# First attention of a four-layer hybrid: the outputs' guard in four passes, two copies on another engine, the queries' rounding and three other steps at other places in the order

## The reference, cut to what matters

```python
h = nan_to_num(layernorm(x), nan=0, posinf=1e4, neginf=-1e4)
Q, K, V = heads(h @ wq.T), heads(h @ wk.T), heads(h @ wv.T)      # 16 heads of 16
Q, K = Q * cos + rotate_half(Q) * sin, K * cos + rotate_half(K) * sin
scores = where(first 25 or last 128 keys, Q @ K.T / 4, lowest)
probs = softmax(scores)
# a gate from the last query's row adds one value to the last values
out = (probs @ V) @ wo.T
x = x + nan_to_num(out, nan=0, posinf=1e4, neginf=-1e4)
```

## Time and profile before

| | us |
|---|---|
| runs, median (lowest to highest of 3) | 941.94 (941.64 to 942.05) |
| the profiled execution | 944.91 |
| its span in the trace | 942.9 |
| busy in the span: TensorE / VectorE / ScalarE / GpSimd | 856.5 / 717.7 / 531.3 / 434.7 |

### The profile page before, as it was taken

How to read it: one execution, slowest core, us unless ns; L and a number is a source line. 1 busy time by engine, 2 the same in 40 slices (tenths; PEclk the granted TensorE clock), 3 DMA queues, 4 the chain that set the end, 5 groups by cost and what they waited for, 6 DMA issues and landing times.

```text
span 942.9 us, 19230 instructions
## 1 busy us (share of the span) xinstructions
PE 856.5 (91%) x6286; PEld 649.1 (69%) x6286; DVE 717.7 (76%) x2366; ACT 531.3 (56%) x1392; POOL 434.7 (46%) x683
## 2 busy tenths in 40 slices
PE   6678898889999999987999999999999997999996
PEld 5556666667765666655888787887888775666663
DVE  6567988889778887663968787787868686888872
ACT  5356544454354555545676676757586761555555
POOL 0348898887766665446202121221202012556655
PEclk9779999999999999989999999999999999999999
DMA  6333333332223557102112020202021022234331
GB/s 211 60 50 49 53 56 55 56 55 38 35 37 58 103 118 133 43 14 46 24 24 46 1 46 1 45 2 46 2 45 37 11 35 35 36 71 59 59 48 35
DMA packets 49938, 46.55 MB, mean 49 GB/s; under 512 B 5280, under 2 KB 47280, under 8 KB 49840
## 3 DMA queue, kind: packets, MB, share of 16 engines
q1 hardware_dynamic: 49840, 45.33, 26.2%
HBM read 11.40 MB, written 2.10 MB: 14 GB/s over the span
## 4 chain that ended last, share of the span: by engine, by line
PE 33%; DVE 15%; issue 3%; ACT 1%; POOL 1%; DMA 0%; POOLq 0%; SPq 0%; DVEq 0%; ACTq 0%
PE bank L301 8%; PE bank L1979 6%; PE bank L1987 4%; PE bank L1913 4%; DVE weights L1476 3%; PE bank L1928 3%; DVE weights L1466 3%; PE bank L1743 2%; PE bank L1756 2%; DVE q_lo L1456 1%; PE bank L1739 1%; DVE rope L1454 1%; PE bank L1782 1%; DVE xn L338 1%; DVE arena L1313 1%
## 5 line engine op out<-in xcount | busy, mean ns | idle before, releaser
L1313 DVE TENSOR_REDUCE arena<-bank 128x2 f32<-128x512 f32 (+1 forms) x192 | 130.9, 685 | 42.4 <-PE bank L1743 41.4
L924 ACT ACTIVATE weights<-bank 128x512 f32<-128x512 f32 x144 | 85.8, 596 | 109.1 <-PE bank L1756 108.3
L1006 ACT ACTIVATE weights<-weights,neg_max 128x128 f32<-128x128 f32 (+1 forms) x256 | 113.9, 449 | 39.2 <-DVE neg_max L1466 38.7
L727 POOL TENSOR_SCALAR_AFFINE_SELECT weights<-weights 128x256 f32<-128x256 f32 x144 | 68.6, 478 | 101.4 <-ACT weights L924 101.4
L1979 PE MATMUL bank<-kbT,arena 128*128 128x128 f32 (+1 forms) x512 | 105.1, 328 | 1.0 <-DVE y L447 0.9
L667 POOL TENSOR_SCALAR weights<-weights 128x512 f32<-128x512 f32 x64 | 97.6, 1537 | 12.5 <-ACT weights L832 12.5
L1743 PE MATMUL bank<-kf_stack,q_stack 96*128 96x256 f32 (+1 forms) x256 | 99.7, 432 | 0.0
L1013 ACT ACTIVATE weights<-bank 128x384 f32<-128x384 f32 x128 | 62.7, 490 | 61.0 <-PE bank L1987 60.5
L1466 DVE CUSTOM_DVE_ANT_0 weights<-bank,arena 128x128 f32<-128x128 f32 (+1 forms) x256 | 80.2, 350 | 14.6 <-PE bank L1979 12.6
L301 PE MATMUL bank<-x_hi,wb_hi 128*128 128x256 f32 x256 | 83.8, 327 | 2.8 <-DVE q_lo L1456 2.8
L1476 DVE TENSOR_SCALAR weights<-weights,inv_sum 128x128 f32<-128x128 f32 (+1 forms) x256 | 81.3, 360 | 4.6
(11 more groups left out here) (236 smaller groups left out, 2514.2 us busy)
## 6 DMA issues: line engine op xcount, KB each, us to landing
q_stack<-q_hi SPq DMA_DIRECT2D x96, 128.0 KB, 4.5
arena<-arena SPq DMA_DIRECT2D x64, 128.0 KB, 2.5
q_stack<-q_lo SPq DMA_DIRECT2D x48, 128.0 KB, 5.3
ka_stack<-k_hi SPq DMA_DIRECT2D x32, 76.5 KB, 2.8
x_all<-x SPq DMA_DIRECT2D x8, 256.0 KB, 5.1
st_wo<-b_wo SPq DMA_DIRECT2D x8, 256.0 KB, 4.2
arena<-b_wqn SPq DMA_DIRECT2D x8, 256.0 KB, 3.3
out<-x_all SPq DMA_DIRECT2D x8, 256.0 KB, 2.1
```

Source lines behind the costliest of these rows:

```text
L924: a.activation(s["pT"][(STEPS * b + k) % N_PT], p2[k % 2][:, :], ACT.Exp).then_inc(s["exp"], 1)
L1006: last = a.activation(p, p, ACT.Exp, scale=-1.0, bias=neg_max[:, h % 4, t:t + 1], accum_out=sums[:, h % 4, t:t + 1])
L1313: v.tensor_reduce(into, p1[k % 2][:, :].rearrange("p (s g k) -> p s g k", s=n, g=NC), AX.X, ALU.max, negate=True).then_inc(s["maxed"], 1)
```

## The change

Eight edits, all in the first attention:

1. The outputs' guard has four passes: the first clamps the bank to +-1e4 into `guard_z`, the second makes max(min(p, 0), `guard_z`) into `guard_t`, the third makes the mask from the bank, the fourth copies the bank where the mask is set. The fourth stands in step 15, the first two in step 13 (step 15 in iteration 9, as before). `ps_r` is held for all four.
2. TensorE's `untranspose_a` and the first `untranspose_f` wait for four passes.
3. The copy into `rep_lo` moves from VectorE to ScalarE, at step 3.
4. The pad of `hT` moves from VectorE to ScalarE, at step 13 ahead of `x_hi`.
5. ScalarE's `high` for the queries moves from step 8 to the end of step 11 for b >= 0.
6. GpSimd's `low` for the queries moves from step 9 to step 12.
7. GpSimd's `residual` moves from step 9 to step 3.
8. SyncE issues `sp_put_shift(b, 0)` at step 10 ahead of the queries' stack, not at step 12 behind it.

Counts and waits of semaphores follow (`guarded` 5 to 4). The core of the diff:

```diff
 # SyncE
+                if k == 10 and there(b):
+                    sp_put_shift(sa, b, 0)
                 if k == 10 and there(b + 1):
                     sp_stack(b + 1, "q")
-                if k == 12 and there(b):
-                    sp_put_shift(sa, b, 0)
 # GpSimd
+                if k == 3 and there(b - 3):
+                    residual(sa, b - 3, guard_t, at(sa, "guarded", b - 3, 4))
-                if k == 9 and b >= 0 and there(b + 1):
+                if k == 12 and b >= 0 and there(b + 1):
                     low(b + 1, "q")
-                if k == 9 and there(b - 3):
-                    residual(sa, b - 3, guard_t, at(sa, "guarded", b - 3, 5))
 # ScalarE
+                if k == 3 and there(b + 1):
+                    act.wait_ge(*at(sa, "x_lo", b + 1, 1))
+                    a.activation(rep_lo[...], x_lo[:, :, 0:VC]..., ACT.Copy).then_inc(sa["rep"], 1)
-                if k == 8 and there(b + 1):
+                if k == 8 and b < 0 and there(b + 1):
                     high(b + 1, "q")
                 if k == 13 and there(b + 2):
+                    act.wait_ge(*at(sa, "hT", b + 2, 2))
+                    act.wait_ge(*at(sa, "x_lo", b + 2, 0))
+                    a.activation(hT[:, :, T:TX], hT[:, :, 0:TX - T], ACT.Copy).then_inc(sa["hT"], 1)
                     act.wait_ge(*at(sa, "hT", b + 2, 3))
-                    act.wait_ge(*at(sa, "x_lo", b + 2, 0))
                 if k % OCT in ITEM_STEPS and there(b - 1):
                     exp_a(b - 1, k // OCT, ITEM_STEPS[k % OCT])
+                if k == 11 and b >= 0 and there(b + 1):
+                    high(b + 1, "q")
 # VectorE
-                link(sa, "guarded", b, 1, v.tensor_scalar(guard_t, ps_r[:, :], 0.0, None, ALU.max))
-                v.scalar_tensor_tensor(guard_z, ps_r[:, :], 0.0, guard_t, op0=ALU.min, op1=ALU.add)\
+                link(sa, "guarded", b, 1, v.tensor_scalar(guard_z, ps_r[:, :], -BIG, BIG, ALU.max, ALU.min))
+                v.scalar_tensor_tensor(guard_t, ps_r[:, :], 0.0, guard_z, op0=ALU.min, op1=ALU.max)\
                     .then_inc(sa["guarded"], 1)
                 if i == 0:
-                    ins = v.tensor_scalar(m, guard_z, 0.0, 0.0, ALU.mult, ALU.is_equal)
-                elif i == 1:
-                    ins = v.tensor_scalar(guard_t, guard_z, -BIG, BIG, ALU.max, ALU.min)
+                    ins = v.tensor_scalar(m, ps_r[:, :], 0.0, 0.0, ALU.mult, ALU.is_equal)
                 else:
-                    ins = v.copy_predicated(guard_t, m, guard_z)
+                    ins = v.copy_predicated(guard_t, m, ps_r[:, :])
-                if k == 3 and there(b + 1):
-                    repeat_lo(b + 1)
-                if k == 6 and there(b - 3):
-                    guard_inf(b - 3, 2)
-                if k == (14 if b <= B else 15) and there(b - 2):
-                    guard_nan(b - 2)
+                if k == (13 if b <= B else 15) and there(b - 2):
+                    guard_nan(b - 2)
 # TensorE
-                    wait_since(pe, sa, "guarded", b - 1, 2)
+                    wait_since(pe, sa, "guarded", b - 1, 4)
```

More of the change, by code:

```diff
@@ L155, in hybrid_layers_kernel @@
                      e_dve=11, e_exp=3, v_ps=1, v_big=1, v_small=1, b_ps=1, v_done=1, rep=2, s_ps=H, maxed=H,
-                     clamped=2, sT_ps=2 * ITEMS, exp=2 * ITEMS, guard=8, guard_first=2, yT_ps=1, yT=1, wo_ps=NT, guarded=5)
+                     clamped=2, sT_ps=2 * ITEMS, exp=2 * ITEMS, guard=8, guard_first=2, yT_ps=1, yT=1, wo_ps=NT, guarded=4)
         sf = [signals("ffn", "f", **TURNED, q_ps=1, kg_ps=2, k_sel=3, k48=3, kT_ps=1, k_stack=1, v_ps=1, v_sel=2,
@@ L881, in step_a @@
                                  ACT.Copy).then_inc(sa["rep"], 1)
+                if k == 3 and there(b + 1):
+                    act.wait_ge(*at(sa, "x_lo", b + 1, 1))
+                    a.activation(rep_lo[:, :, :].rearrange("p c (g k) -> p c g k", g=G),
+                                 x_lo[:, :, 0:VC].bitcast(f32).unsqueeze(2).to_broadcast([P, NC, G, VC]),
+                                 ACT.Copy).then_inc(sa["rep"], 1)
                 if k == 5 and there(b - 2):
@@ L1180, in turn_x @@
                 link(sa, "hT", b, 1, v.tensor_scalar(h_pos[:, :, :], halves(ps_a), 0.0, BIG, ALU.max, ALU.min))
[L1181 to L1191, removed]
+                v.scalar_tensor_tensor(hT[:, :, 0:T], halves(ps_a), 0.0, h_pos[:, :, :], op0=ALU.min, op1=ALU.add)\
+                    .then_inc(sa["hT"], 1)
             def last_row_least(b):
@@ L1288, in step_a @@
                     last_row_least(b + 1)
+                if k == (13 if b <= B else 15) and there(b - 2):
+                    guard_nan(b - 2)
                 if k == (14 if b <= B else 15) and there(b - 2):
-                    guard_nan(b - 2)
-                if k == 15 and there(b - 2):
                     guard_inf(b - 2, 0)
@@ L1792, in untranspose_f @@
                     pe.wait_ge(*at(s, "oT", b, o + 1))
-                    pe.wait_ge(*(at(sa, "guarded", B - 1, 2) if s is sf[0] and (b, o) == (0, 0) else at(s, "y", b, 3 * o)))
+                    pe.wait_ge(*(at(sa, "guarded", B - 1, 4) if s is sf[0] and (b, o) == (0, 0) else at(s, "y", b, 3 * o)))
                     if o == 0 and there(b + 1):
```

## The result

The changed kernel takes 958.38 us (median of four runs, 952.89 to 959.10) against 942.0: a ratio of 1.0155 [1.0113, 1.0197], 16.4 us more. The forecast was slower by 4.7, with a range that ended at 950.0. The sign is right, the size is not. The profiled execution took 958.11 (span 956.4, against 942.9).

What follows compares the result with a forecast made beforehand. No engine was full in the first attention; order and waits, mostly the queries' landing, set the pace. 6.6 − 1.8 = 4.8, prologue +0.4, end +0.5, relief −1.0 gave +4.7: 946.6 us on the median, forecast range 944 to 949.5, overall 941.5 to 950.

Steps and rivals of the forecast that it cites:

- M9: Start of VectorE's maximum of step 9, the iteration's clock; forecast 0.5 us earlier, bounds 0 and 1.14.
- faster rival: Queries' copies land as fast as issued, not needing 8.6 us; about 935.5 us; chance 0.17.
- its step 12 costs nothing: Queries' low part on GpSimd, moved to step 12: no cost; uncovered it would add up to 1.5 us.
- The end of the stage: Turning of outputs at the first attention's end waits for two more guard passes, about 1.4 us later: +0.5.
- Prologue: rep_lo's copy on ScalarE sends batch 0's keys and queries out later: +0.4 us.
- The rival that counts VectorE's whole relief: M9 comes 1.14 us earlier in iterations 3 to 5, 0.25 in 0 to 2; 943.6 us, the same; chance 0.15.
- the clock was a rival: TensorE's clock falls in longer stops ahead of score 0; about 0.5 us more per start, 950 us; chance 0.08.
- +4.8: Sum over iterations 0 to 6: 6.6 us lost by later q_hi, less 1.8 gained in iterations 3 to 5.
- SP's order: Two small shift copies stand ahead of the queries on SP's queue: no cost taken, 0.3 us at most.
- a part of 1.0: Relief from fewer VectorE passes in batches 7 to 9, perhaps 1.0 us given back.
- second rival: The rival that counts VectorE's whole relief: three iterations gain 3.7 us, four lose 5.4; 943.6 us; chance 0.15.
- the 0.4 of iteration 2: rep_lo's copy on ScalarE, which has no pause in iteration 2, makes k_hi, rstd and M9 0.4 us later.

Runs made afterwards that it cites:

- e4: Changed kernel plus eight unread 128x256 matmuls on TensorE ahead of score 0 of batches 1 to 7, filling the stops: 950.14 us, ratio 1.0075.
- e6: Changed kernel with SP's two shift copies back behind the queries and eight unread matmuls ahead of score 0 of batches 1 to 7: 946.13 us, ratio 1.0033.
- e3: Changed kernel with only SP's order undone, the shift copies back at step 12 behind the queries: 953.41 us, ratio 1.0114.
- e8: e5 plus two to eight unread matmuls ahead of score 0 of batches 0, 1, 2, 3, 6 and 7: 935.65 us, ratio 0.9918.
- e5: Changed kernel with queries rounded at ScalarE's step 10, low part at GpSimd's step 9, shift copies behind the queries: 937.38 us, ratio 0.9948.

## Why the prediction was right in sign and wrong in size

**Right.**
- All of batches 1 to 7 start on the DMA: 31.1 us of waiting with batch 0's (15 or more was said), and each score 0 follows its landing by 0.04.
- q_hi starts 1.70 to 1.71 behind M9 in iterations 1 to 5 (said: 1.8). In iteration 6 it moves from 0.17 ahead of M9 to 2.14 behind it, 2.3 us (said: 1.9). With the stops filled (e4) iteration 1 leaves the pattern: M9 comes 1.2 sooner behind the first maximum than before, but q_hi, held by exponentials that wait for TensorE's products, starts 3.27 behind it. Iteration 4 of the changed kernel, maximum and rounding:

```profile
162.21 0.46 DVE L1148 TENSOR_REDUCE arena<-bank 128x2 f32<-128x306 f32 x1
```

```profile
163.92 0.62 ACT L839 ACTIVATE q_hi<-arena 128x512 fp32r<-128x512 f32 x1
```

- The copies need 8.33 to 8.79 us from first issue to last landing (said: 8.6). The faster rival is out: here the four copies of the high part took longer to issue than the 2.48 of the earlier trace rows, and the last landing still came 8.77 behind the first issue. The 0.3 us a copy in that rival came from a ceiling; each of these copies writes 16 partitions only (`row:row + HD`), and no run varies that: the rows show that these copies are slower than the estimate, and don't test the ceiling. SP's queue in that iteration:

```profile
164.63 3.68 SPq L421 DMA_DIRECT2D q_stack<-q_hi  x4
168.35 1.26 SPq L421 DMA_DIRECT2D q_stack<-q_lo  x2
```

  The low part is issued directly behind the high part, so its step 12 costs nothing, as said.
- The end of the stage: the turning of outputs waits for the two further passes, and the next projection starts when x_lo is there. Timeline of DVE, then of PE:

```profile
301.54 0.73 DVE L1132 COPY_PREDICATED arena<-arena,bank 128x512 f32<-128x512 int32 x1
302.16 0.68 DVE L357 TENSOR_TENSOR x_lo<-bank,x_hi 128x512 fp32r<-128x512 f32 x1
```

```profile
302.37 0.63 PE L434 MATMUL bank<-cst,oT 128*128 128x128 f32 x4 [2.04 <-issue]
302.89 0.39 PE L301 MATMUL bank<-x_hi,f_hi 128*128 128x256 f32 x1
```

  The stop is 2.04 instead of 0.55, 1.5 longer (said: 1.4), and guard and x_lo together take 3.47 instead of 3.02: +0.45 (said: +0.5).
- Prologue: score 0 of batch 0 at 33.34, against 33.16: +0.2 (said: +0.4).
- The rival that counts VectorE's whole relief needs M9 1.14 sooner. At full clock (e4) M9 stands 15.06, 15.20 and 15.21 behind the first maximum in batches 3, 4 and 5, where it stood 15.15, 15.70 and 15.49: 0.1, 0.5 and 0.3 sooner (said: 0.5), and in batches 4 and 5 of e4 VectorE waits 0.91 for rstd instead of 0.61 (said: 1.2; in the changed kernel itself it is 0.28). It is out too.

**Wrong, first: the clock was a rival, and was priced too low.** The sum held the clock at nothing; as a rival I gave it 0.08 and "about 0.5 us more each", 3.4 in all. Filling the stops gives back 8.2 us of the medians; at the end of batch 7 it is 9.5 in the profiles (252.7 against 243.2). Per start that is more than twice my price. And it belonged in the sum: the rival itself put 2 to 4 us of waiting ahead of each score 0 (measured: 3.4 to 4.7), and the earlier trace rows showed 0.84 in the stretch that followed batch 1's stop of 1.95. Its reading of these rows was wrong in one point, though: batch 4 had no stop ahead of it (its score 0 ran 1.44 behind the landing), and batch 2, behind a stop of 1.32, ran at 1.00. So the rows raised the question and had no price for it. What the forecast says by itself, batches at the clock that they had, was nearly right: +6.6 with the stops filled over batches 0 to 6, against +4.8.

**Wrong, second: "No cost taken, 0.3 at most" for SP's order.** The sum compared end times in the usual iteration (M9 + 2.4 on both sides) and did not ask in which iteration VectorE does something else ahead of L375. In iterations 2 and 3 the copies went out 0.65 and 0.80 later. That is most of the 1.8 by which the filled sum misses the forecast: with the shift copies behind the queries (e6) batch 2's period changes by +1.8 and batch 3's by −0.2, where +2.0 and −0.6 were said. What is left in batch 3 is M9, 0.1 sooner and not 0.5. By itself the order costs 1.3 in batches 2 and 3 (e4 against e6). Without the filling it is 3.5 in the stage (e3, one profile of each), and 2.2 of that lie in batches 1 and 7, where the order delays no copies: they are 1.0 and 1.2 shorter in e3, where TensorE leaves the lower clock 3.8 and 5.8 us behind score 0, not 6.1 and 8.6.

**By sums**, at the end of batch 7: 15.2 later. Of it 9.5 goes with the filled stops, so it is the clock's (less what the filling itself costs), 1.3 is SP's order, and the 4.4 that stay are near the 5 that the forecast had up to there (4.8 and 0.4, less a part of 1.0). Of the 1.3, e6 shows 0.4 at the end of batch 7, since its filling outlasts two stops; by e6 alone 5.3 stay. The medians' 16.4 hold 1.2 more than the 15.2, the spans 1.7 less. What lies behind batch 7 moves by that much without an edit: e8 reaches the end of batch 7 4.0 sooner than e5 (228.7 and 232.7), and their spans are 934.3 and 934.4, with 20.3 and 8.0 us at the lower clock in the rest. Why the lower clock falls there more often in one than in the other is not settled.

Two figures of the prediction don't follow from its own terms, and neither bears on the miss. The forecast's range, 946.6 with −1.9 and +1.5 and 1 more at each end, is 943.7 to 949.1 and not 944 to 949.5. And the four batches that lose in the second rival lose 5.85 (6.6 less three times 0.25); its 5.4 needs the 0.4 of iteration 2 to be left out as well, which it doesn't say.

## What to carry to other kernels

When an edit makes the fullest engine wait some us at the same place in each iteration, count the work behind that wait at the lower clock from the start, as a part of the forecast: here 9.5 of the 15.2 us at the end of the stage went when the stops were filled. In an issuing queue whose entries wait in order, ask for each iteration, not for the usual one, what the entry that is now in front waits for. And undo an edit's parts one by one: three moves of this change cost 17 to 20 us, its other parts gained 3.5, and a rounding one step earlier, with the other two moves undone, kept the gain. Where the whole varies by some us that no edit explains, measure at the end of the stage that was edited, and look at the granted clock behind it.

## What I had not expected of the hardware

Useless matmuls on the fullest engine made a kernel 8.2 us faster (958.4 to 950.1): with 3.4 to 4.7 us of stop ahead of each batch TensorE ran 66 of 207 us at 1.2 GHz, with the stops filled 21. The same idea on the kernel before, whose stops were short, cost 4.2 us (941.8 to 946.0) at an unchanged mean of 0.92. And a stop alone doesn't decide: e5 waits for its queries twice as long as the kernel before (16.3 us against 8.3) at the same mean clock. Behind its stops of 2.12 and 2.38 us (batches 2 and 7) the first 5 us ran at 1.00, behind 1.98 and 1.63 (batches 3 and 6) at 0.66.
